# A graph-attention layer on one core: the carry row between edge pairs kept in PSUM, destination rows repeated in DRAM

## What is computed

```python
q = (feat @ Wq.T + bq).reshape(n, H, HD); k = ...; v = ...
score = jnp.einsum('ehd,ehd->eh', q[edge_dst], k[edge_src])
score = jnp.clip(score / math.sqrt(HD), -10.0, 10.0)
ex = jnp.exp(score - smax[edge_dst])
den = jax.ops.segment_sum(ex, edge_dst, num_segments=n)
wv = jax.ops.segment_sum((ex / den[edge_dst])[:, :, None] * v[edge_src], edge_dst, num_segments=n)
x = feat + wv @ Wp.T + bp
h = _layernorm(x, ln_g, ln_b)
h = jax.nn.gelu(h @ W1.T + b1, approximate=False) @ W2.T + b2
out = _layernorm(feat + x + h)
```

## Time and profile before

| | |
|---|---|
| median of 3 runs | 1255.74 us (1253.55 to 1261.97) |
| the profiled execution | 1265.42 us, its span 1263.5 us |
| mean granted TensorE clock | 0.861 of full speed |
| PE busy | 1024.3 us (81%) |
| DVE busy | 1015.2 us (80%) |
| POOL busy | 744.0 us (59%) |
| ACT busy | 518.5 us (41%) |

### The profile page before, as it was taken

The page is one execution under the profiler, slowest core; times in us unless marked ns, Lnnn a source line. Parts: engine busy times, 40 slices in busy tenths (PEclk is TensorE's granted clock), DMA queues, the critical chain, the costliest instruction groups (busy, mean ns, idle before and its releaser), DMA issues.

```text
span 1263.5 us, 24619 instructions
## 1 busy us (share of the span) xinstructions
PE 1024.3 (81%) x5924; PEld 655.2 (52%) x5924; DVE 1015.2 (80%) x1777; ACT 518.5 (41%) x1257; POOL 744.0 (59%) x801
## 2 busy tenths in 40 slices
PE   7883558978888887888788788887887988988887
PEld 6761225545555554554455455455554545545565
DVE  4865768978887898888889788888888888877943
ACT  2120224444444454544445454443443444444432
POOL 0007777777666666776766676667666666666000
PEclk9996567978988898998989789789789788878989
DMA  7777898888778878887887787787787788778210
GB/s 239 252 254 231 290 299 267 253 275 272 240 235 256 252 237 255 267 242 229 280 254 240 241 267 238 236 266 246 223 258 245 225 248 252 233 247 255 78 31 27
DMA packets 159157, 298.02 MB, mean 236 GB/s; under 512 B 34584, under 2 KB 95447, under 8 KB 159064
## 3 DMA queue, kind: packets, MB, share of 16 engines
q0 software_dynamic: 62560, 205.05, 52.1%
q1 hardware_dynamic: 96504, 92.04, 23.2%
HBM read 261.85 MB, written 35.13 MB: 235 GB/s over the span
## 4 chain that ended last, share of the span: by engine, by line
PE 29%; DMA 22%; DVE 19%; SPq 15%; issue 12%; POOL 1%; ACT 1%; DVEq 0%; ACTq 0%; POOLq 0%
DMA agg_rows<-acc_sb 12%; DMA agg_in<-agg_rows 6%; SPq L508 5%; PE bank L402 5%; DVE score L1288 5%; PE bank L354 5%; SPq L515 5%; PE quad L748 5%; PE quad L789 4%; DVE prod L1281 3%; PE bank L778 3%; DVE ev L1301 2%; SPq L472 2%; DMA staged<-agg_rows 2%; DVE stats L412 1%
## 5 line engine op out<-in xcount | busy, mean ns | idle before, releaser
L321 POOL DMA_INDIRECT kv<-kv_rows,src_sb x782 | 741.0, 948 | 426.1 <-issue 222.3
L1281 DVE TENSOR_TENSOR prod<-kv,quad 128x1024 f32<-128x1024 f32 x196 | 239.3, 1221 | 25.5 <-DMA kv<-kv_rows,src_sb 23.4
L789 PE MATMUL quad<-qwin,onehotT 32*128 32x256 f32 x1568 | 163.4, 490 | 118.0 <-DVE prod L1281 112.6
L1288 DVE TENSOR_REDUCE score<-prod 128x32 f32<-128x1024 f32 x196 | 237.8, 1213 | 1.6
L1301 DVE TENSOR_TENSOR ev<-kv,bank 128x1024 f32<-128x1024 f32 x196 | 238.0, 1214 | 0.5 <-ACT ev L1004 0.5
L402 PE MATMUL bank<-w_sb,hid 128*128 128x256 f32 x736 | 200.2, 428 | 0.0
L789 PEld LDWEIGHTS quad<-qwin,onehotT 32*128 32x128 f32 x1568 | 71.8, 213 | 216.8 <-issue 122.6
L382 PE MATMUL bank<-hT,w_sb 128*128 128x256 f32 x736 | 182.2, 392 | 0.4 <-ACT hid L390 0.4
L402 PEld LDWEIGHTS bank<-w_sb,hid 128*128 128x128 f32 x736 | 157.3, 219 | 30.5 <-issue 5.6
L382 PEld LDWEIGHTS bank<-hT,w_sb 128*128 128x128 f32 x736 | 139.0, 194 | 34.0 <-ACT hid L390 10.3
L798 PE MATMUL bank<-ev,onehot 128*32 128x264 f32 x1568 | 142.5, 439 | 5.3 <-ACT acc_sb L1018 3.7
(11 more groups left out here) (104 smaller groups left out, 1043.1 us busy)
## 6 DMA issues: line engine op xcount, KB each, us to landing
dst_rows<-edge_dstT SPq DMA_DIRECT2D x200, 64.0 KB
kv_rows<-kv_out SPq DMA_DIRECT2D x25, 512.0 KB, 3.0
qwin<-q_rows SPq DMA_DIRECT2D x392, 32.0 KB
kv<-kv_rows,src_sb POOLq DMA_INDIRECT x782
agg_rows<-acc_sb SPq DMA_DIRECT2D x98, 82.5 KB
xT_sb<-xT SPq DMA_DIRECT2D x25, 256.0 KB, 3.9
xq_sb<-xT SPq DMA_DIRECT2D x25, 256.0 KB
agg_in<-agg_rows SPq DMA_DIRECT2D x24, 264.0 KB
```

The costliest lines, as they stand in the source:

```text
L321: return nc.gpsimd.indirect_dma_start(out=rows, out_offset=None, in_=kv_dram, in_offset=bass.IndirectOffsetOnAxis(ap=index, axis=0))
L789: last = nc.tensor.matmul(quad[:, i, 0:C], onehotT[rows, slot // 2, cols], qwin[rows, slot // 2], start=True, stop=True)
L1281: nc.vector.tensor_tensor(prod[:, slot % 2].rearrange("p (i c) -> p i c", c=C), kv[:, slot, :, 0:C], quad[:, :, 0:C], ALU.mult).then_inc(s ...
L1288: nc.vector.tensor_reduce(score[:, slot % 2], prod[:, slot % 2].rearrange("p (h d) -> p h d", d=HD), AX.X, ALU.add).then_inc(s_score, 1)
```

## The change

The carry doesn't go through DRAM any more. `place` gets two buffers. Its columns 32 to 127 hold the merge matrix, so that the 80 summed rows stand in PSUM rows 32 to 111 (`FIRST_OUT`), columns 1 to 31 are zero, and column 0 picks the row of the next pair's base (`carry_all`, worked out once for all pairs): the merge puts the carry into row 0 and zeros into rows 1 to 31 of `bank4`. The next pair's sums of tile 0 accumulate on that (`start=False`). ACT writes column 0 for each pair (`select_carry`), in the even slot after the copy of the pair before. `load_carry` is gone. The array of destination rows is repeated 32 times in DRAM, so one DMA of 128 rows takes the place of four.

```diff
@@ SP
             def load_destination_rows(turn, t):
-                for i in range(TILES):
-                    sp.dma_start(dst_rows[WIN * i:WIN * (i + 1), t],
-                                 edge_dstT[i:i + 1, bass.ds(turn * (SLOTS * P) + t * (HALF_TURN * P), HALF_TURN * P)]
-                                 .broadcast_to([WIN, HALF_TURN * P])).then_inc(s_drow[t], 16)
+                cols = bass.ds(turn * (SLOTS * P) + t * (HALF_TURN * P), HALF_TURN * P)
+                sp.dma_start(dst_rows[:, t], edge_dstT[:, cols]).then_inc(s_drow[t], 16)
-            def load_carry(p, slot):
-                sp.wait_ge(s_aggst, 16 * p)
-                base = pair_base(p)
-                sp.dma_start(staged[P - 1:P, slot % 2], agg_dram[bass.ds(base, 1), :]).then_inc(s_carry, 16)
-
             def store_sums(p, slot):
+                base = pair_base(p)
                 sp.wait_ge(s_accc, p + 1)
                 if exists(p - 1, PAIRS):
                     sp.sem_inc(s_gate_sp, 1)
                     sp.wait_ge(s_aggst, 16 * p)
-                base = pair_base(p)
-                sp.dma_start(agg_dram[bass.ds(base, STORE_ROWS), :], acc_sb[0:STORE_ROWS, slot])\
+                sp.sem_inc(s_gate_sp, 1)
+                sp.dma_start(agg_dram[bass.ds(base, STORE_ROWS), :], acc_sb[FIRST_OUT:FIRST_OUT + STORE_ROWS, slot])\
                     .then_inc(s_aggst, 16)
@@ SP, edges
-                    if i % 2 == 0 and exists(done, PAIRS) and exists(done - 1, PAIRS):
-                        load_carry(done, (i // 2 + 2) % 4)
@@ PE
             def merge(p, slot):
                 pe.wait_ge(s_stc, p + 1)
-                if exists(p - 1, PAIRS):
-                    pe.wait_ge(s_carry, 16 * p)
-                nc.tensor.matmul(bank4[:, 0:ACC], place[:], staged[:, slot % 2], start=True, stop=True)\
+                pe.wait_ge(s_csel, p + 1)
+                nc.tensor.matmul(bank4[:, 0:ACC], place[:, slot % 2], staged[:, slot % 2], start=True, stop=True)\
                     .then_inc(s_mrg, 1)
@@ PE, sums
-                                            start=(slot % 2 == 0), stop=(slot % 2 == 1))
+                                            start=(slot % 2 == 0 and (i > 0 or not exists(p - 1, PAIRS))),
+                                            stop=(slot % 2 == 1), skip_group_check=(i == 0))
@@ ACT
-                nc.scalar.activation(staged[0:P - 1, slot % 2], bank4[0:P - 1, 0:ACC], ACT.Copy).then_inc(s_stc, 1)
+                nc.scalar.activation(staged[:, slot % 2], bank4[:, 0:ACC], ACT.Copy).then_inc(s_stc, 1)
+            def select_carry(p, slot):
+                nc.scalar.activation(place[:, slot % 2, 0:1], carry_all[:, bass.ds(p, 1)], ACT.Copy).then_inc(s_csel, 1)
@@ ACT, edges
                         copy_sums(done, (i // 2 + 2) % 4)
+                    if i % 2 == 0 and exists(done + 1, PAIRS):
+                        select_carry(done + 1, (i // 2 + 3) % 4)
@@ DVE, once
+                nc.vector.tensor_scalar(carry_all[:], base_rise[:], place_row[:], None, ALU.is_equal)\
+                    .then_inc(s_rise, 1)
+                for b in range(2):
+                    nc.vector.memset(place[:, b, 0:FIRST_OUT], 0.0)
+                    nc.vector.tensor_scalar(place[:, b, FIRST_OUT:P], iota_row[:, 0:P - FIRST_OUT], place_row[:], None,
+                                            ALU.is_equal).then_inc(s_place, 1)
```

More of the change, by code:

```diff
@@ L19 @@
 STORE_ROWS = 80
+FIRST_OUT = WIN
 CLIP = 10.0
@@ L83, in gnn_program @@
         place_row = sb("place_row", [P, 1])
-        place = sb("place", [P, P])
-        merge_row = sb("merge_row", [P, 1])
+        place = sb("place", [P, 2, P])
         minus_start = sb("minus_start", [P, PAIRS])
@@ L106, in gnn_program @@
         base_rise = sb("base_rise", [P, PAIRS])
+        carry_all = sb("carry_all", [P, PAIRS])
         parts = sb("parts", [P, 3, PAIR_TILES + 1])
@@ L211, in gnn_program @@
         s_mrg = sem("pairs_merged")
-        s_carry = sem("carry_row_in")
+        s_csel = sem("carry_column_ready")
         s_accc = sem("sums_copied")
@@ L542, in store_q_unit, with store_sums @@
                     .then_inc(f_qst, 16)
-            def load_carry(p, slot):
-                sp.wait_ge(s_aggst, 16 * p)
+            def store_sums(p, slot):
                 base = pair_base(p)
-                sp.dma_start(staged[P - 1:P, slot % 2], agg_dram[bass.ds(base, 1), :]).then_inc(s_carry, 16)
-            def store_sums(p, slot):
                 sp.wait_ge(s_accc, p + 1)
@@ L704, in _ @@
             pool.wait_ge(s_placer, TILES)
-            nc.gpsimd.affine_select(out=merge_row[:], in_=place_row[:], compare_op=ALU.not_equal, fill=0.0,
-                                    base=1 - P, pattern=[[0, 1]], channel_multiplier=1).then_inc(s_placer, 1)
             nc.gpsimd.affine_select(out=ident[:], in_=ident[:], compare_op=ALU.not_equal, fill=1.0,
@@ L889, in _ @@
             pe.wait_ge(s_const, 9)
-            pe.wait_ge(s_place, 1)
+            pe.wait_ge(s_place, 2)
             pe.wait_ge(s_kvb, 2 * UNITS)
@@ L985, in transposed_onehots @@
             def transposed_onehots(p, slot, uses):
-                act.wait_ge(s_drow[slot // 2], 64 * uses)
+                act.wait_ge(s_drow[slot // 2], 16 * uses)
                 if exists(p - 1, PAIRS):
@@ L1106, in _ @@
             act.wait_ge(s_start, 1)
+            act.wait_ge(s_rise, 2)
+            act.wait_ge(s_place, 2)
             for p in range(2):
@@ L1196, in locate @@
                     .then_inc(s_rise, 1)
-                dve.wait_ge(s_placer, TILES + 1)
-                nc.vector.tensor_scalar(place[:], iota_row[:], merge_row[:], None, ALU.is_equal).then_inc(s_place, 1)
+                dve.wait_ge(s_rise, 1)
+                nc.vector.tensor_scalar(carry_all[:], base_rise[:], place_row[:], None, ALU.is_equal)\
[4 more added lines that the diff above has]
+                                            ALU.is_equal).then_inc(s_place, 1)
             def check_edges():
@@ L1223, in check_edges @@
                 dve.wait_ge(s_chk, 5)
-                nc.vector.tensor_scalar(margins[:, 3:4], margins[:, 1:2], -1.0, float(WIN - 2), ALU.mult, ALU.add)\
+                nc.vector.tensor_scalar(margins[:, 3:4], margins[:, 1:2], -1.0, float(WIN - 1), ALU.mult, ALU.add)\
                     .then_inc(s_chk, 1)
@@ L1408, in edges @@
                         scores(n, i)
-            nc.vector.memset(staged[:], 0.0)
             dve.wait_ge(s_iota, 1)
@@ L1548 @@
         "edge_dst": tiles_dst.T,
-        "edge_dstT": rows_dst.transpose(1, 0, 2).reshape(TILES, -1),
+        "edge_dstT": np.repeat(rows_dst.transpose(1, 0, 2).reshape(TILES, -1), WIN, axis=0),
         "bases": bases[None],
```

## The result

The changed kernel takes 1162.72 us (median of 4 runs, 1153.05 to 1164.58), the kernel before 1257.08 us beside it; the ratio is 0.923 with a 95% interval of 0.917 to 0.929. The forecast was 1140 us in a range of 1128 to 1190.

What follows compares the result with a forecast made beforehand. VectorE was taken as the bound, with POOL's gathers close behind. Waits of 80.5, 32 and 2 us, limited to 112 us near POOL's floor, plus 4 us of tail, took the 1255.7 us median to 1140; range 1128 to 1190.

Steps and rivals of the forecast that it cites:

- `den`'s wait: VectorE's division waiting for a block's node sums: 80.5 of 88.0 us gained by SP's earlier store and load (bounds 37, 80.5).
- The residual's wait: VectorE's residual waiting for TensorE's projection at the lower clock: 32 of 37.6 us gained (bounds 0 and 37).
- The output sum: VectorE's output sum waiting for the feed-forward product: place unchanged, 2 of 10.8 us gained (bounds 0 and 10).
- Which limit then holds: Last batch's product: VectorE at 1082, POOL's gathers at 1075 to 1077, taken as 1084; gain to there 112 us.
- The carry wait on TensorE: TensorE's merge waiting 43.4 us for the carry: gone, but counted as nothing because TensorE is not the bound.
- The tail: After the last product: store out sooner and TensorE's queue started sooner, 4 us gained (bounds 2 and 6).
- Added work: 98 small ACT instructions, 19 us in all, and a few on VectorE: costed at nothing.
- Denser transfers: Rival: DMA transfers slow down as they get denser, half of the gain, 1184 us; chance 0.22.
- The clock as a rival: Rival: the projection on TensorE still runs at 1.2 GHz, the 32 us stay, 1172 us; chance 0.08.
- The others: Rivals: little change as the store leaves no earlier, about 1250 us, 0.04; slower through late q windows, 0.04.

Runs made afterwards that it cites:

- dummy_carry_c: The changed kernel, carry in PSUM, with SP's old waits and a load of an unused row ahead of the q windows; 1252.86 us, ratio 0.986.
- filler run: The changed kernel with 10 matmuls that nobody reads on TensorE in slot 6 of each full turn; 1149.44 us, ratio 0.9125.

## Why the prediction was right or wrong

- *`den`'s wait, 80.5 us gained.* Right in size: all of it is gone. The chain was drawn a little too short: I let the node sums be asked for at 4.5 us behind the store, they are at 5.06. SP also issues the output rows and the four windows, and its list has 2.4 us of waits for landed stores at this load, in 3 places; in the other turns its own issues come last. The spare time is smaller than the 1.8 us forecast: with 4.90 us for the load, as in the forecast, the sums are there at 693.41, 0.56 us ahead of `den` at 693.97 (an estimate). It was enough.
- *The residual's wait, 32 of 37.6 us.* Right; 36 are gone, with the stall ahead of it. dummy_carry_c bears out the cause: there `den` waits again, and so does the residual, 35.7 us.
- *The output sum, 2 of 10.8 us gained.* This is the term that failed: 15.7 us lost, 17.7 us off. I wrote that the place "doesn't change". But the pause at VectorE's norm steps, with the lower clock behind it, now makes the output sum wait 1.3 to 1.6 us in each turn from 435 us on; before, such a wait came in a few turns only. The filler run shows that it is the clock: with the pause filled the wait is gone and the time is 1149, 13 us less and 9 us above the forecast. Why the place was mostly free of it before is not shown; that TensorE was held up at other places of the turn instead is my reading.
- *Which limit then holds.* POOL's floor of 1.25 us a gather was right, and the filler version runs on it. In the changed kernel VectorE's path with the output sum's wait, 41.0 us a turn, lies above it, so POOL was the next bound and not the first. The last product came at 1100, not at 1084; most of the 16 us are the term above.
- *The carry wait on TensorE "counts nothing by itself".* The number came out, and for the kernel before the traces don't contradict it: two thirds of its merges didn't wait. But the sum of terms left out a condition. It books the 80.5 us at `den` to SP's order and gives the carry no price; by the same sum the order alone would have gained about 80 us. The run gave no gain: `den`'s wait fell to 9.6 us and the merge's rose from 43.4 to 149.8. Removing the carry's way through DRAM is what lets the gain at `den` through. That the change did both at once made the sum right; in this part there was luck in it.
- *The tail, 4 us.* 5.2 us measured.
- *Added work.* The new instruction on ACT took 0.19 us:

```profile
669.15 0.19 ACT L1012 ACTIVATE place<-carry_all 128x1 f32 x1
```

  Nothing on VectorE waits for it. Right.
- *The rivals.* Denser transfers: the DMA share in a steady turn rose from 0.79 to 0.87, at 275 GB/s, and `den` didn't wait; it didn't happen. The Trainium skill, "DMA: Bandwidth & Descriptors", "Latency and other measured facts", gives the HBM's access latency as 0.2 us on average and 2 us at high load. The waits of the changed kernel show no such growth at the higher share. The clock as a rival was placed at the projection; it turned up at the output sum instead, at 15.7 us where 32 had been priced. The others didn't happen.

## What to carry to other kernels

A wait that recurs once in a turn is worth its sum only if no second path comes up close behind it. Here one chain (store, SP's queue, node sums, division) and one loop (store, landing, carry, merge) ran through the same stores: order alone gave 1.012, the carry alone with the old waits 0.986, both together 0.923. To find such a second path, follow what goes from one iteration to the next through DRAM and ask at each step who waited for whom. Adding up the steps from start to start doesn't tell, since they always make the period. And after stalls are removed, read again where TensorE pauses: here a pause of 3 us ahead of a product that VectorE waited for was filled with matmuls that compute nothing, and the kernel took 13 us less.

## What the runs showed of the hardware

- The stalled TensorE costs twice: 3.21 us of idle time, then twelve products in 4.56 us at a granted clock of 0.60, and in 2.76 us when ten matmuls that compute nothing (2.50 us) stand in the gap. The mean clock of the turn is 0.92 and 1.00. The Trainium skill, "TensorE: Matmul & The Clock Gate", "What's actually happening", names the throttled state as the default which activity releases; the trace agrees, with work that computes nothing as the activity.
- While VectorE holds none back for more than 0.3 us, POOL issues an indirect gather each 1.26 us (982.9 us for 781 steps in the changed kernel, 0.947 us of it busy).
- The same program takes about 1260 us on two chips and 1589 to 1620 us on three others, where 295 to 363 us of the products' waits are ended by nothing that the profile can name. The whole change wasn't run on those three.
